# Adapter factors gathered by pairs of samples, and the order of the work at the first turn, at a change of pair and in the last unit of an attention pipeline

## What is computed

```
x = x + L0(x)   gated MLP, 1376 inner features, each of W_gate, W_up, W_down with an adapter of rank 16
x = x + L1(x)   x W^T + bias + scale[adapter] * ((x A^T) B^T)     rank 16, one of 8 adapters
x = x + L2(x)   x W^T + bias + 2 * ((x A) B)                      rank 16, one of 32 adapters
x = x + L3(x)   attention: 32 query heads and 8 key heads of 128, RMS norm and rotary
                embedding on q and k, 512 cached keys in pages (masked by cache_seqlens) and the
                128 new ones, softmax, output projection to 512
```

## Time and profile before

| | |
|---|---|
| median of 3 runs | 1333.03 us (1332.83, 1333.03, 1337.01) |
| profiled execution: its time | 1333.57 us |
| its span | 1332.0 us |
| mean granted TensorE clock, share of full | 0.992 |
| instructions | 25952 |
| PE busy, matmuls | 1297.4 us, 6728 |
| DVE, ACT, POOL busy | 972.5, 779.8, 756.7 us |

### The profile page before, as it was taken

One profiled execution on the slowest core, in us unless ns is written; L12 is line 12 of the kernel. 1 busy time (PEld: TensorE's weight loads), 2 busy tenths in 40 slices (PEclk: granted clock), 3 DMA queues, 4 the chain that ended last, 5 costly groups with the idle time before them and its releaser, 6 DMA issues.

```text
span 1332.0 us, 25952 instructions
## 1 busy us (share of the span) xinstructions
PE 1297.4 (97%) x6728; PEld 1102.7 (83%) x6728; DVE 972.5 (73%) x2500; ACT 779.8 (59%) x1829; POOL 756.7 (57%) x778
## 2 busy tenths in 40 slices
PE   8999999997999999999999999999999999999997
PEld 8888888886888888788888878888888787888886
DVE  5532344978778877978777788888777878777883
ACT  5731334455566667576666666666566666656663
POOL 3100000257666668776666686766667876666662
PEclk9999999998999999999999999999999999999998
DMA  7321214176555557756555577555557665555533
GB/s 259 130 63 48 71 48 128 52 261 185 121 123 122 125 127 199 182 124 136 127 132 128 141 186 188 121 134 139 131 120 182 178 159 116 121 122 122 122 90 79
DMA packets 314845, 178.01 MB, mean 134 GB/s; under 512 B 260752, under 2 KB 279568, under 8 KB 314512
## 3 DMA queue, kind: packets, MB, share of 16 engines
q1 hardware_dynamic: 296128, 126.88, 39.9%
q0 software_dynamic: 11264, 32.77, 9.8%
q10 hardware_dynamic: 7376, 17.45, 4.0%
HBM read 118.15 MB, written 16.91 MB: 101 GB/s over the span
## 4 chain that ended last, share of the span: by engine, by line
PE 79%; DVE 6%; ACT 4%; issue 4%; POOL 2%; SPq 2%; DMA 1%; ACTq 0%; DVEq 0%; POOLq 0%
PE bank L1555 15%; PE tail L1593 15%; PE wide L1623 12%; PE tail L1657 11%; PE wide L455 4%; PE wide L1587 4%; PE wide L531 3%; PE bank L1576 3%; PE bank L455 2%; PE tail L455 2%; PE wide L583 2%; DVE parts L1968 1%; PE bank L531 1%; ACT prT L1758 1%; POOL wq1T L1303 1%
## 5 line engine op out<-in xcount | busy, mean ns | idle before, releaser
L1593 PE MATMUL tail<-prT,vt 128*128 128x512 f32 x960 | 266.3, 416 | 8.9 <-POOL prT L1349 2.8
L1593 PEld LDWEIGHTS tail<-prT,vt 128*128 128x128 f32 x960 | 173.8, 193 | 55.5 <-DVE prT L1957 12.5
L1286 POOL TENSOR_TENSOR tick<-tick 128x1 f32<-128x1 f32 x254 | 55.8, 220 | 270.6 <-PE tail L1593 91.6
L1657 PE MATMUL tail<-woT,oT 128*128 128x512 f32 x768 | 179.7, 390 | 0.8 <-DVE oT L2008 0.8
L1657 PEld LDWEIGHTS tail<-woT,oT 128*128 128x128 f32 x768 | 144.1, 188 | 31.1 <-DVE oT L2008 1.2
L1623 PE MATMUL wide<-kT,qT 128*128 128x320 f32 x512 | 158.8, 310 | 2.0 <-DVE mx L1984 1.5
L1623 PE MATMUL wide<-kT_low,qT 128*128 128x320 f32 x512 | 158.4, 309 | 0.0
L1623 PE MATMUL wide<-kT,qT_low 128*128 128x320 f32 x512 | 158.1, 309 | 0.0
L1786 ACT ACTIVATE pr<-pr,nm,q_scale 128x640 f32<-128x640 f32 x128 | 118.0, 922 | 42.7 <-DVE nm L1987 42.2
L1786 ACT ACTIVATE raw<-raw,nm,q_scale 128x640 f32<-128x640 f32 x124 | 114.7, 925 | 44.7 <-DVE nm L1987 43.5
L1340 POOL TENSOR_TENSOR parts<-raw,parts 128x1280 f16<-128x1280 f32 x50 | 132.4, 2647 | 7.3
(11 more groups left out here) (280 smaller groups left out, 2912.4 us busy)
## 6 DMA issues: line engine op xcount, KB each, us to landing
w_ring<-pair_weights SPq DMA_DIRECT2D x80, 256.0 KB, 4.3
k_raw<-k_pages SPq DMA_DIRECT2D x512, 32.0 KB, 1.7
v_raw<-v_pages SPq DMA_DIRECT2D x512, 32.0 KB, 2.8
spread<-one_over_denominators ACTq DMA_DIRECT2D x32, 512.0 KB, 4.6
xTb<-x_transposed POOLq DMA_DIRECT2D x31, 512.0 KB, 4.2
rope<-rope_tables SPq DMA_DIRECT2D x31, 256.0 KB, 2.8
out<-y POOLq DMA_DIRECT2D x31, 256.0 KB, 4.9
w_raw<-w_gate_up SPq DMA_DIRECT2D x10, 512.0 KB, 3.3
```

The lines of the kernel that those rows point to most:

```text
L1286: nc.gpsimd.tensor_tensor(tick[:, 2:3], tick[:, 1:2], tick[:, 1:2], ALU.add).then_inc(s_carry, 1)
L1593: last = nc.tensor.matmul(tail[g][:, :], vt[v_part][:, j, g * D:(g + 1) * D], prT[p_part][:, :, j, :], start=(j == v_part == p_part == 0), ...
L1657: last = nc.tensor.matmul(place[:, :], oT[:, g, o_part, (h % REP) * S:(h % REP + 1) * S], woT[w_part][:, h, :], start=(h == o_part == w_pa ...
```

## The change

- **A.** `b_rows` works by pairs of samples: for each pair one matmul of 256 columns that holds the high and low rows of two samples, so two of 256 columns in place of two of 512. The gathers are four for each factor, each factor's rows have their own place (in tiles that are used up by then), and POOL waits for `s_actlo` ahead of b1 and b2. `high_rows` is one copy, `low_rows` two subtractions, `high_tail` three copies with a wait on itself, `low_tail` two subtractions.
- **B.** In turn (0, 0) POOL casts both pairs of heads first, makes both rests itself (DVE made four), then the values' low part alone (ACT makes the high part), the turned second parts, and only then the weight chunks 12 to 17. SP sends the two first parts ahead of the two second ones, and all four ahead of the stores of x. ACT takes the new keys and values from PSUM at head 5, not at head 7, which lets them wait in `qk` and `tail[0]`.
- **C.** In unit 0 of a new pair PE does the output share ahead of wq1's projection. In the turn before ("next") POOL makes weight chunks 8 to 11 together, behind both casts and the rest of heads 2 and 3, which DVE made before. SP sends the first parts ahead.
- **D.** In "out" of pairs 1 to 3 POOL makes the rest of heads 2 and 3 (DVE before), and then weight chunks 17 to 19 (17 and 18 stood between the casts).
- **E.** In the last turns, DVE makes the rest of heads 2 and 3 of unit 31; PE transposes all new probabilities ahead of its wait for the turned ones, and does all high sums, then the low ones; ACT's and DVE's copies of the new probabilities wait for those.

```
@@ adapters: PE, ACT, DVE, POOL
-                    for c in range(2):
-                        gather(rows_raw[:, c, :], row_half[:, i, c:c + 1], a[name], s_rraw[i])
+                        pool.wait_ge(s_actlo, FT + (2, 8)[i - 1])
+                    for q in range(B // 2):
+                        gather(rows_raw[i][:, q, :], row_pair[:, i, q:q + 1], a[name], s_rraw[i])
...
+                def b_pairs(stage, h, b, begins):
+                    c = stage % 2
+                    for q in range(2):
+                        last = nc.tensor.matmul(quarter(stage, h)[:, q * 2 * S:(q + 1) * 2 * S], b[:, 2 * c + q, h * P:(h + 1) * P], th[:, c, q, :],
+                                                start=(begins and q == 0), stop=(not begins and q == 1))
+                    return last
+
                 def b_rows(stage, h, b):
-                    c = stage % 2
-                    for part in range(2):
-                        last = nc.tensor.matmul(quarter(stage, h), b[:, c, part, h * P:(h + 1) * P], th[:, c, part, :],
-                                                start=False, stop=(part == 1))
-                    last.then_inc(s_grp, 1)
+                    b_pairs(stage, h, b, False).then_inc(s_grp, 1)
...
-                    ac.copy(th[0:4 * R, stage % 2, 0, :], tm[0:4 * R, stage % 2, :]).then_inc(s_thih, 1)
-                    ac.copy(th[:, stage % 2, 1, :], tm[:, stage % 2, :]).then_inc(s_thih, 1)
+                    c = stage % 2
+                    ac.copy(th[:, c], tm_of[:, c]).then_inc(s_thih, 1)
+                    act_e.wait_ge(s_thih, 2 * stage + 1)
+                    for q, to in enumerate((6 * R, 4 * R)):
+                        last = ac.copy(th[to:to + 2 * R, c, q, :], tm_of[2 * R * q:2 * R * (q + 1), c, q, :])
+                    last.then_inc(s_thih, 1)
@@ SP: turn_probs
+            for k, i in ((0, 0), (1, 0), (0, 1), (1, 1)) if firsts_ahead else ((0, 0), (0, 1), (1, 0), (1, 1)):
@@ POOL: turn
                 pool.wait_ge(s_step, u * NSTEP + MASKED)
-                low_weights(own, 3 * KT, 3 * KT + 3)
+                halve(u, n, 0, True, False)
                 for i in range(2):
                     pool.wait_ge(m_full[i], B // 2)
                 pool.wait_ge(s_xlast, 16 * (B // 4))
-                halve(u, n, 0, True, False)
-                split_values(u, n + 1, True)
-                halve(u, n + 2, 1, True, False)
-                low_weights(own, 3 * KT + 3, 4 * KT)
+                halve(u, n + 1, 1, True, False)
+                for k in range(2):
+                    make_rest(u, k, True)
+                split_values(u, n + 2, False)
             else:
                 split_values(u, n, not extra)
                 if extra == "next":
                     low_weights(own, 6, 8)
+                halve(u, n + 1, 0, False, not extra)
+                if extra == "out":
+                    low_weights(own, 4 * KT, 4 * KT + 1)
+                halve(u, n + 2, 1, False, then_x is not None)
+                if extra == "next":
+                    low_weights(own, 2 * KT, 3 * KT)
                 elif extra == "out":
-                    low_weights(own, 4 * KT, 4 * KT + 1)
-                halve(u, n + 1, 0, False, not extra)
-                if extra == "next":
-                    low_weights(own, 2 * KT, 2 * KT + 2)
-                elif extra == "out":
-                    low_weights(own, 4 * KT + 1, 4 * KT + 3)
-                halve(u, n + 2, 1, False, not extra)
-                if extra == "next":
-                    low_weights(own, 2 * KT + 2, 3 * KT)
-                elif extra == "out":
-                    low_weights(own, 4 * KT + 3, NCHUNK)
+                    low_weights(own, 4 * KT + 1, NCHUNK)
             low_turned(u, n + 3, 0)
+            low_turned(u, n + 4, 1)
             if first_turn:
+                low_weights(own, 3 * KT, 4 * KT)
                 pool.wait_ge(s_init[1], 16 * BLK)
                 low_weights(own, 4 * KT, LEFT[0])
-            low_turned(u, n + 4, 1)
@@ PE: turn
-            if front:
+            shares_first = share and first_turn
+            if front and not shares_first:
                 project(0, wqT[1], ready=chunks_done(pair, 2 * KT) if first_turn else None)
...
                 output(tail[1], w, REP, REP).then_inc(s_y, 1)
+            if front and shares_first:
+                project(0, wqT[1], ready=chunks_done(pair, 2 * KT))
+            if back and not front:
+                for w in range(2):
+                    probs_wide(1, w)
+                transposes(0, probs_of(1, JT - 1))
...
-                sums(0, range(JT), (0, 1), 0)
-                sums(0, (0, 1), (0,), 1)
-                probs_wide(1, 0)
+                highs = sums(0, range(JT), (0, 1), 0)
+                if front:
+                    sums(0, (0, 1), (0,), 1)
+                    if not share:
+                        begin(0)
+                    probs_wide(1, 0)
+                else:
+                    highs.then_inc(s_ph, 1)
+                    sums(0, range(JT), (0,), 1).then_inc(s_pv, 1)
@@ ACT: new_keys_values and scores
+                    ac.copy(qk[:, :, :], bank[0][:, G * D:2 * G * D].rearrange("p (h d) -> p h d", d=D)).then_inc(s_vheld, 1)
...
-                    if ahead and h == (REP + 1 if back else HP - 1):
+                    if ahead and h == REP + 1:
                         full0.n = (TURN if back else FRONT)[0]
                         new_keys_values(n + 1)
@@ DVE: scores
-                    if (extra or not back) and h in (REP + 1, HP - 1):
+                    if back and extra and h == REP + 1:
                         for i in range(HALF):
-                            rest_of((h - REP - 1) // 2 * HALF + i)
+                            rest_of(i)
+                    if back and not ahead and h == HP - 1:
+                        for i in range(HALF, REP):
+                            rest_of(i)
```

139 lines of the change are left out of this document (87 added, 52 removed).

## The result

The changed kernel has a median of 1337.13 us (20 runs, 1333.97 to 1338.72), the kernel before 1334.94 us in 20 runs beside it (1330.17 to 1338.20). The ratio is 1.0021 with a 95% interval of 1.0011 to 1.0030: slower by 0.2%, less than what the prediction called measurable. Forecast were 1321.4 us and a range of 1312.5 to 1327.0.

A forecast was written before the change was run, and what follows sets the result against it. TensorE, busy 97% of the span, was taken as the bound: matmuls, standstills and halved clock. Terms −3.6 − 5.0 + 2.4 − 0.5 − 4.9 = −11.6 us gave 1322.0 profiled, 1321.4 as median; range 1312.5 to 1327.

The forecast's parts named there:

- the pair costs POOL a fifth only: At pair changes, POOL's pair of weights beside DVE's rests was taken as 1.2 times as long, not fully blocked.
- Part A: Adapter factors by pairs in the head: −5.2 us of matmuls, partly given back, −3.6 net; range −5.2 to −2.5.
- 0.8 given back: Third stage of the head: DVE's slack of 1.9 us against PE being 2.6 earlier, so some 0.8 comes back.
- Part B: First turn: projection starts at once, sums at 317.2 and not 323.15; −5.0 us, range −5.8 to −3.5.
- the rotated keys: for that I take 1.0 off: First turn, behind the sums: the keys end a DVE chain freed less early, so 6.0 us gained becomes 5.0.
- Part C: New pairs' first turns: sums 0.6 us earlier, low clock 1.6 more; +0.8 each, +2.4 for three.
- The gap that was put at 3.5: New pairs' first turns: 3.5 us from projection's end to sums, no longer covered by the output share.
- rival 2: The clock holds at the pair changes: 3 × 1.4 us less, 1317.2; chance 0.20.
- Part D: Units 1 and 2 of new pairs: output-weight waits of 1.9, 1.9, 2.4 us, other waits gone; −0.5 net.
- Rival 3: The clock falls in unit 2's turns too, from one wait of 1.9 us: 2 × 2.1 more, 1325.6; chance 0.12.
- Part E: Last unit: transposes fill PE's 2.79 us wait and sums run at full clock; −4.9 us, range −5.5 to −3.
- Rival 4: Slower, POOL bounds the pair changes, instructions 1.2 times as long beside DVE: 17.4 us in all, 1338.8; chance 0.07.

The follow-up runs named there:

- experiment 5: Changed kernel with the last factor's row low parts moved from DVE to POOL, and POOL's first weights waiting for masked activations' low parts; 1343.01 us, ratio 1.0065.
- Experiment 1: Changed kernel with POOL's low parts of weight chunks 12 to 17 moved from the first turn to the next, behind the keys; 1336.08 us, ratio 1.0022.
- experiment 6: Changed kernel with chunks 12 to 15 made in POOL's first-turn idle time, 16 to 19 in the next turn; 1329.92 us, ratio 0.9968.
- experiment 8: Changed kernel with the edits of experiment 5, experiment 6 and edit 7 together; 1327.77 us, ratio 0.9951.
- experiment 10: Changed kernel with edit 7, experiment 9's edit, and first-turn weights as two ahead of the first cast, one between, five next turn; 1319.59 us, ratio 0.9896.
- the five others named in the result: Profiles of five follow-up kernels with the changed kernel's code in the pairs' units 0 to 2; unit 0's turns sum to 105.4 us in one, 106.6 to 107.1 in four.
- experiment 11: Changed kernel with part C undone; 1340.79 us, ratio 1.0054 to the kernel before.
- experiment 9: Changed kernel with the last factor's rows copied by ACT and subtracted by DVE in idle time between second and third stages' tails; 1334.49 us, ratio 1.0010.
- edit 7: Changed kernel with output weight chunks 16 and 17 made earlier, in POOL's idle time behind unit 1's keys, in pairs 1 to 3; 1330.18 us, ratio 0.9970.
- experiment 2: Changed kernel with part D undone; 1333.70 us, ratio 1.0000 to the kernel before.

## Why the prediction was wrong

**The reading of the port.** The prediction took the Trainium skill's rule that GpSimd and DVE exclude each other ("SBUF — State Buffer", section "SBUF: two separate sides": the loser fully blocks) and set against it that "the pair costs POOL a fifth only". That is the first step that failed, and the largest: the first turn's error and a third of the head's come from it. The price was read on POOL's side alone, where one short DVE operation gets in per instruction. On DVE's side an operation that is shut out waits for the rest of POOL's: 0.17 becomes 1.20. The rows to see it were there: the two rests of 4.76 us in the earlier trace rows ran beside POOL's low part of the values, and alone one takes 0.81. The trace agrees with the rule, also in that a DVE operation with one input in memory is shut out (experiment 5). The Trainium skill names for that case DVE's two-port mode; whether these operations run in it no row shows.

**Part A** (−3.6, measured −0.4). The saving of 5.2 is real. The slack of 1.9 at the third stage was counted without the rows' second piece (+1.24, an edit that was named and given no price: a piece on 32 partitions costs as much as one on 64) and without what two pieces cost beside POOL's pair of subtractions, which one piece had passed at no cost (+1.0), so 0.8 given back became 2.2, and the low clock behind it took 1.6. The 0.8 was the step, and the reason was that a tail "cut into more pieces" got no number. That the clock may fall in the head was not in the forecast.

**Part B** (−5.0, measured +1.7). The start of the projection (308.4, forecast 308.9) and the start of the sums (317.08, forecast 317.2) came out; two small misses cancel in the latter, as POOL's chain ended at 316.26 and the four transposes stand between it and the sums. The failed term is "the rotated keys: for that I take 1.0 off"; measured 4.29 of waiting, and 2.3 more in the matmuls behind it at the low clock. What was left out: weights 12 to 17, which the change moved behind the turned lows, were moved past DVE's chain; part B's account has no term for them. Experiment 1 took them away: −6.9 us, a first turn of 33.2, which is the forecast's −5.0 (38.4 to 33.4) to 0.2. So the mechanism was right up to this one collision. But these weights must be made somewhere: in experiment 1 the next turn paid 3.9 for them, and experiments 6, 8 and 10, with some of them in POOL's gaps, have both turns short.

**Part C** (+2.4, measured −1.0). The form was right: a wait in one piece behind the projection, the clock falling in some. In pair 1 the sums start 12.65 us behind the turn's start (547.13 − 534.48), where 13.11 was forecast and 13.69 stood before. The gap that was put at 3.5 is 2.9. (The sum on record doesn't close: 542.8 + 3.2 is 546.0, not 546.3.) It was sized as if the clock always fell; in two of three here it didn't, and rival 2 (the clock holds, −0.6 each) describes pairs 2 and 3 (−0.8 each). The gain of this one profile is luck: in the five others named in the result the three turns together are 0.1 to 1.8 us longer than before, four of them 1.3 or more, which is nearer to the forecast. The forecast also took the clock of 1.00 at 533 to 541 as given for the old order; experiment 11 has the old order with the clock fallen in two of three pairs, and with part C undone the median is 3.7 higher. So what the term left out is that the order it was set against can lose its clock too.

**Part D** (−0.5, measured +4.6). The place and the mechanism were right: PE waits for POOL's output weights, 3.28, 2.08 and 2.97, against 1.9, 1.9 and 2.4. Undersized were the wait for the last output weight (in pair 1 POOL's chain began 7.9 us ahead of the turn in place of 8.9, and it waited twice 0.2 for ACT's exponentials, which it had not reached before) and above all the clock, which fell behind it in pair 1: 2.9 us. Rival 3 named this, with a chance of 0.12. It is not the wait's length alone that decides: in experiment 9 the same wait of 3.28 us in pair 1 left the clock at 1.00 (the share took 5.6), and the turn took 34.73.

**Part E** (−4.9, measured −4.5) held, each step to 0.4 us.

**The whole.** Rival 4, POOL as the bound at the pair change, had its place right for unit 2 and wrong for the first turn, where most of the error lies: of the 12.0 us between −11.6 and +0.4, the first turn has 6.7, part D 5.1, the head 3.2, part E 0.4, and part C gave 3.4 back.

## What to carry to other kernels

Before work is moved on POOL, look at what DVE does in the same microseconds: a back-to-back row of POOL subtractions turned small DVE steps of 0.17 us into steps of 1.2, and a chain of such steps is the worst place to put it. Give POOL's movable work to the moments in which it idles and DVE isn't on the critical path, and count its length up to the next thing that is due, as edits 6, 7 and 9 do. Where TensorE waits two to three us, count the matmuls behind the wait at both clock levels: with the same code and the same wait the clock fell in some profiles here and held in others. For the same reason a part's worth is not to be read from one profile.

## What was not expected of the hardware

- DVE operations of 0.17 us take 1.19 to 1.21 us behind POOL subtractions of 1.24 us, one for each; with POOL idle they take 0.17. Operations of DVE that read from PSUM beside POOL's subtractions kept their time (0.82 us, at 305.85 and 307.42 in the changed kernel). So did some small ones from memory to memory: the reciprocal of 128x8 (0.20 us at 607.23) and the transpose of 128x32 (0.21 at 607.46) ran in the middle of POOL's subtractions of 605.66 to 609.39. POOL's casts shut out as well: steps of 0.17 took 1.30 and 1.10 us beside two casts of 1.26 (at 609.45 and 611.20).
- A POOL subtraction of 32 partitions by 1024 takes 2.56 us, one of 128 by 512 1.24 to 1.29; on DVE 32 by 1024 takes 1.22, as 64 by 1024 did (1.21). Fewer partitions save nothing on either engine.
- Waits of PE of 1.92 and 0.29 us left the granted clock at 1.00 in the changed kernel's pair 2, and 1.92 and 0.25 brought it down in pair 3 of experiment 9; 3.28 us brought it down in the changed kernel and left it at 1.00 in experiment 9. In experiment 2, 0.86 and 0.75 in a row brought it down in pair 1, and 0.84 and 0.79 did not in pair 2.
